# Loading x turned by DMA instead of turning it on TensorE, in an attention and mixture-of-experts kernel

## The reference, cut to what matters

```
x = x + xattn(layernorm(x), k, bias, ctx, ctx, 8)
xt = layernorm(x).reshape(2048, 256)
scores = softmax(xt @ Wg.T)                    # 16 experts in 4 groups
topi = the 4 best experts within the 2 best groups
h = silu(xt @ W1[e].T) * (xt @ W3[e].T)        # 176 wide, for each chosen expert e
y = sum over the 4 of scores[e] * (h @ W2[e].T)
z = the same with shared weights, 352 wide, for every token
x = x + y + z
```

## Time and profile before

| what | us |
|---|---|
| median of 3 runs | 399.13 |
| lowest, highest | 397.67, 399.59 |
| the profiled execution's span | 395.4 |
| TensorE busy | 384.7 |
| VectorE busy | 244.1 |
| GpSimd busy | 180.3 |
| ScalarE busy | 162.9 |

### The profile page before, as it was taken

The page is one execution under the profiler, slowest core; times in us unless marked ns, Lnnn a source line. Parts: engine busy times, 40 slices in busy tenths (PEclk is TensorE's granted clock), DMA queues, the critical chain, the costliest instruction groups (busy, mean ns, idle before and its releaser), DMA issues.

```text
span 395.4 us, 9070 instructions
## 1 busy us (share of the span) xinstructions
PE 384.7 (97%) x2146; PEld 279.3 (71%) x2147; DVE 244.1 (62%) x676; ACT 162.9 (41%) x494; POOL 180.3 (46%) x225
## 2 busy tenths in 40 slices
PE   6999999999999999999999999999999999999996
PEld 6788888888888546555667675446767777777765
DVE  3577577987988465788735344443445464646466
ACT  5347656564564362101124333333333333334431
POOL 3254323337888573565553333333333333334333
PEclk9999999999999999999999999999999999999999
DMA  7974474368879996256376873334474737362737
GB/s 248 363 254 139 163 277 144 133 206 278 309 250 335 414 419 258 96 207 223 104 215 219 321 239 107 87 95 134 127 246 136 242 115 242 115 232 103 264 97 251
DMA packets 37812, 83.09 MB, mean 210 GB/s; under 512 B 5930, under 2 KB 25870, under 8 KB 35728
## 3 DMA queue, kind: packets, MB, share of 16 engines
q1 hardware_dynamic: 31248, 64.83, 49.1%
q0 software_dynamic: 6528, 17.84, 11.6%
HBM read 60.21 MB, written 23.48 MB: 212 GB/s over the span
## 4 chain that ended last, share of the span: by engine, by line
PE 79%; DVE 10%; DMA 4%; issue 2%; ACT 2%; SPq 1%; DVEq 1%; POOL 0%; POOLq 0%
PE heads L1382 18%; PE bank L1456 13%; PE heads L1271 11%; PE heads L1424 7%; PE heads L1273 5%; PE bank L1437 5%; PE heads L1392 4%; PE bank L1403 4%; PE bank L1285 3%; DVE kv L734 3%; PE heads L1374 3%; DMA toep<-toep_in 2%; PE bank L1448 2%; DVE prod L763 2%; DMA y_scratch<-toep,dest_i 2%
## 5 line engine op out<-in xcount | busy, mean ns | idle before, releaser
L716 POOL DMA_INDIRECT y_scratch<-toep,dest_i x72 | 71.8, 997 | 112.0 <-DVE dest_i L1131 96.0
L1382 PE MATMUL heads<-experts,toep 128*128 x256 | 86.6, 461 | 0.6 <-DVE toep L1089 0.5
L1271 PE MATMUL heads<-toep,kv 128*128 128x256 f32 x256 | 77.9, 386 | 1.9 <-DVE kv L734 0.8
L661 POOL DMA_INDIRECT rows_scratch<-rows,slot_i x64 | 63.3, 989 | 35.4 <-issue 19.5
L1456 PE MATMUL bank<-experts,toep 88*128 x256 | 66.2, 381 | 1.6 <-DVE toep L1096 1.6
L553 ACT ACTIVATE toep<-heads 128x176 f32<-128x176 f32 x72 | 22.8, 317 | 78.1 <-PE heads L1382 67.2
L1382 PEld LDWEIGHTS heads<-experts,toep 128*128 128x128 f32 x256 | 43.7, 190 | 14.8 <-issue 1.1
L1273 PEld LDWEIGHTS heads<-toep,kv 128*128 128x128 f32 x256 | 48.7, 190 | 6.5
L763 DVE TENSOR_TENSOR prod<-heads,ctx_rep 128x1024 f32<-128x1024 f32 x32 | 39.1, 1221 | 22.3 <-PE bank L1285 19.9
L1096 DVE COPY toep<-heads 88x256 f32<-88x256 f32 x72 | 30.2, 419 | 31.1 <-PE heads L1392 31.1
L1273 PE MATMUL heads<-toep,kv 128*128 128x128 f32 x256 | 49.2, 274 | 0.0
(11 more groups left out here) (240 smaller groups left out, 513.4 us busy)
## 6 DMA issues: line engine op xcount, KB each, us to landing
ctx_rep<-ctxr_in SPq DMA_DIRECT2D x16, 1024.0 KB, 5.0
experts<-experts_in SPq DMA_DIRECT2D x16, 608.0 KB
toep<-rows_scratch SPq DMA_DIRECT2D x56, 144.0 KB
prod<-y_scratch SPq DMA_DIRECT2D x5, 1024.0 KB, 5.5
rows_scratch<-pad_row SPq DMA_DIRECT2D x17, 144.0 KB, 1.8
ctx_tr<-ctxt_in SPq DMA_DIRECT2D x16, 128.0 KB
toep<-toep_in SPq DMA_DIRECT2D x4, 512.0 KB, 7.0
ctx_n<-ctx_in SPq DMA_DIRECT2D x16, 128.0 KB, 2.1
```

Source lines behind the costliest of these rows:

```text
L661: pool.indirect_dma_start(rows_d, bass.IndirectOffsetOnAxis(ap=slot_i[:, u, k:k + 1].bitcast(U32), axis=0), rows[:, u, :], None).then_inc( ...
L716: pool.indirect_dma_start(y_d, bass.IndirectOffsetOnAxis(ap=dest_i[b][:, 0:1].bitcast(U32), axis=0), y_sb[b], None, bounds_check=TOPK * TO ...
L1271: nc.tensor.matmul(y_ps[par][:, i, :], kv[:, q, 0, h * P:(h + 1) * P], toep[:, q * HH + h, :], start=True, stop=False)
L1382: last = nc.tensor.matmul(up_ps[p], x_tr[p][:, blk, :], up_w(e, blk), start=blk == 0, stop=blk == LB - 1)
```

## The change

The rows are scattered in another layout, and loaded turned.

- After `norm2`, which now writes into `xn`, ScalarE runs one more instruction for each unit (`split_row`): it splits the 256 float32 numbers of a row into 256 lower and 256 upper halves of 16 bits, side by side in `rows`. The scatter moves the same 1152 bytes per row.
- `gather` issues a DMA transpose of the 128 rows x 512 halves, which lands as 4 blocks of 128 x 128 halves, and a second, plain DMA of the 32 gates per row, with a semaphore of its own. A mixed tile takes two of each, a late tile one of each.
- `turn_x` on TensorE is gone, and its PSUM banks. `src_tr` on ScalarE no longer copies from PSUM but weaves the lower and upper halves in SBUF into float32, 512 halves per partition, and waits for the DMA instead of for TensorE.

```
+            def turned(mem, at, lo, count):
+                return sp.dma_start_transpose(in_halves(mem).rearrange("p (r n) -> p r n", n=P)[:, :, lo:lo + count],
+                                              halves_d[bass.ds(at, count), 0:2 * L])
             def gather(t, b, before):
                 if not (isinstance(t, int) and t < DEPTH):
-                    sp.wait_ge(xtr_ps, t - (DEPTH - 1))
+                    sp.wait_ge(xtr_ready, t - (DEPTH - 1))
                     sp.wait_ge(taken, t - (DEPTH - 1))
...
                 if is_mixed(t):
-                    sp.dma_start(xg[b][0:HALF], rows_d[bass.ds(at, HALF)]).then_inc(rows_in[b], 16)
+                    turned(xg[b], at, 0, HALF).then_inc(rows_in[b], 16)
+                    sp.dma_start(xg[b][0:HALF, L:], rows_d[bass.ds(at, HALF), L:]).then_inc(gates_in[b], 16)
...
                 else:
-                    sp.dma_start(xg[b], rows_d[bass.ds(at, P)]).then_inc(rows_in[b], 16)
+                    turned(xg[b], at, 0, P).then_inc(rows_in[b], 16)
+                    sp.dma_start(xg[b][:, L:], rows_d[bass.ds(at, P), L:]).then_inc(gates_in[b], 16)
...
+            def split_row(u):
+                act.wait_ge(xn_ready, u + 1)
+                nc.scalar.activation(in_halves(rows[:, u, :]).rearrange("p (s l) -> p s l", s=2),
+                                     xn_of(u).bitcast(U16).rearrange("p (l s) -> p s l", s=2), ACT.Copy
+                                     ).then_inc(row_ready, 1)
...
-            def src_tr(w, p):
+            def src_tr(w, p, b, before):
                 if not (isinstance(w, int) and w < 2):
                     act.wait_ge(up_done, w - 1)
-                act.wait_ge(xtr_ps, w + 1)
-                nc.scalar.activation(x_tr[p], xt_ps[p], ACT.Copy).then_inc(xtr_ready, 1)
+                rows_landed(act, w, b, before)
+                nc.scalar.activation(x_tr[p].rearrange("p b n -> p (b n)").bitcast(U16).rearrange("p (n s) -> p n s", s=2),
+                                     in_halves(rows_of(w, b)).rearrange("p (s n) -> p n s", s=2), ACT.Copy
+                                     ).then_inc(xtr_ready, 1)
...
             def routed_step(t, b, before):
                 up(t, p, b)
-                if not (isinstance(t, int) and t == LIVE - 1):
-                    turn_x(t + 1, 1 - p, (b + 1) % DEPTH, before + 1 if b == DEPTH - 1 else before)
```

More of the change, by code:

```diff
@@ L27 @@
 I32 = mybir.dt.int32
+U16 = mybir.dt.uint16
 U32 = mybir.dt.uint32
@@ L102, in build @@
         resid = sb("resid", [P, UNITS, L])
+        xn = sb("xn", [P, L])
         rows = sb("rows", [P, UNITS, ROW])
@@ L110, in build @@
         ident = sb("ident", [P, P])
+        blocks = xn[:, 0:P]
         sum_i = sb("sum_i", [P, 2, 32])
-        blocks = sb("blocks", [P, P])
         skip_w = sb("skip_w", [P, 2, P])
@@ L221, in build @@
         s_up, s_silu, s_hid, s_down = sem("shared_up"), sem("shared_silu"), sem("shared_hid"), sem("shared_down")
-        rows_in = [sem(f"rows_in{b}") for b in range(DEPTH)]
-        xtr_ps, xtr_ready, up_done, silu_done, hid_ready, ht_done, htr_ready, dn_done = (
-            sem("xtr_ps"), sem("xtr_ready"), sem("up_done"), sem("silu_done"), sem("hid_ready"), sem("ht_done"),
+        rows_in, gates_in = ([sem(f"{n}_in{b}") for b in range(DEPTH)] for n in ("rows", "gates"))
+        xtr_ready, up_done, silu_done, hid_ready, ht_done, htr_ready, dn_done = (
+            sem("xtr_ready"), sem("up_done"), sem("silu_done"), sem("hid_ready"), sem("ht_done"),
             sem("htr_ready"), sem("dn_done"))
@@ L227, in build @@
         y_sent = [sem(f"y_sent{b}") for b in range(DEPTH)]
-        late_in = [sem(f"late_in{j}") for j in range(LATE)]
+        late_in, late_gates = ([sem(f"{n}{j}") for j in range(LATE)] for n in ("late_in", "late_gates"))
         sends_ready, unit_ps, unit_ready = sem("sends_ready"), sem("unit_ps"), sem("unit_ready")
@@ L232, in build @@
         other_in = [sem(f"other_in{g}") for g in range(MIXED)]
-        others_in = [sem(f"others_in{b}") for b in range(DEPTH)]
+        others_in, other_gates = ([sem(f"{n}{b}") for b in range(DEPTH)] for n in ("others_in", "other_gates"))
         added, finished = sem("added"), sem("finished")
@@ L237, in build, with xn_of @@
         block = ctx.enter_context(nc.Block())
+        def xn_of(u):
+            return spread[:] if u == UNITS - 1 else xn[:]
         def v_forward(q):
@@ L274, in rows_of, with in_halves @@
             return rows[:, UNITS - LIVE + t, :] if is_late(t) else xg[b]
+        def in_halves(mem):
+            return mem[:, 0:L].bitcast(U16)
         def rows_landed(eng, t, b, before):
@@ L281, in rows_landed, with gates_landed @@
                 eng.wait_ge(rows_in[b], before * 16 + 16)
+            if is_mixed(t):
+                eng.wait_ge(others_in[b], (t - MIXED0) // DEPTH * 16 + 16)
+        def gates_landed(eng, t, b, before):
+            if is_late(t):
+                eng.wait_ge(late_gates[t - LIVE + LATE], 16)
+            else:
+                eng.wait_ge(gates_in[b], before * 16 + 16)
+            if is_mixed(t):
+                eng.wait_ge(other_gates[b], (t - MIXED0) // DEPTH * 16 + 16)
         def is_mixed(t):
@@ L363, in gather @@
                 if is_mixed(t):
-                    sp.dma_start(xg[b][0:HALF], rows_d[bass.ds(at, HALF)]).then_inc(rows_in[b], 16)
+                    turned(xg[b], at, 0, HALF).then_inc(rows_in[b], 16)
+                    sp.dma_start(xg[b][0:HALF, L:], rows_d[bass.ds(at, HALF), L:]).then_inc(gates_in[b], 16)
                     also = sp.value_load(other_row[0:1, t - MIXED0:t - MIXED0 + 1], min_val=0, max_val=E * REGION + HALF)
-                    sp.dma_start(xg[b][HALF:P], rows_d[bass.ds(also, HALF)]).then_inc(others_in[b], 16)
-                else:
-                    sp.dma_start(xg[b], rows_d[bass.ds(at, P)]).then_inc(rows_in[b], 16)
+                    turned(xg[b], also, HALF, HALF).then_inc(others_in[b], 16)
+                    sp.dma_start(xg[b][HALF:P, L:], rows_d[bass.ds(also, HALF), L:]).then_inc(other_gates[b], 16)
+                else:
+                    turned(xg[b], at, 0, P).then_inc(rows_in[b], 16)
+                    sp.dma_start(xg[b][:, L:], rows_d[bass.ds(at, P), L:]).then_inc(gates_in[b], 16)
             def load_other(g):
@@ L409, in late_gather @@
                 at = sp.value_load(tile_row[0:1, t:t + 1], min_val=0, max_val=E * REGION)
-                sp.dma_start(rows[:, UNITS - LATE + j, :], rows_d[bass.ds(at, P)]).then_inc(late_in[j], 16)
+                mem = rows[:, UNITS - LATE + j, :]
+                turned(mem, at, 0, P).then_inc(late_in[j], 16)
+                sp.dma_start(mem[:, L:], rows_d[bass.ds(at, P), L:]).then_inc(late_gates[j], 16)
             others_at = {5: (0,), 7: (1,), 8: (2,), 9: (3,), 10: (4,), 11: (5,), 13: (6,), 14: (7,)}
@@ L501, in norm2 @@
                 act.wait_ge(b2, u + 1)
-                nc.scalar.activation(rows[:, u, 0:L], resid[:, u, :], ACT.Identity,
-                                     bias=ln2[:, u, 4:5], scale=ln2[:, u, 3:4]).then_inc(row_ready, 1)
+                if 1 <= u < UNITS - 1:
+                    act.wait_ge(xt_done, u)
+                nc.scalar.activation(xn_of(u), resid[:, u, :], ACT.Identity,
+                                     bias=ln2[:, u, 4:5], scale=ln2[:, u, 3:4]).then_inc(xn_ready, 1)
+            def split_row(u):
[3 more added lines that the diff above has]
+                                     ).then_inc(row_ready, 1)
             def copy_xn(u):
@@ L538, in _ @@
                     norm1(u + 2)
+                if u >= 2:
+                    split_row(u - 2)
                 if u >= ROUTE0 and (u - ROUTE0) % TB == 0:
                     exponentials((u - ROUTE0) // TB)
-            def src_tr(w, p):
+            def src_tr(w, p, b, before):
                 if not (isinstance(w, int) and w < 2):
                     act.wait_ge(up_done, w - 1)
-                act.wait_ge(xtr_ps, w + 1)
-                nc.scalar.activation(x_tr[p], xt_ps[p], ACT.Copy).then_inc(xtr_ready, 1)
+                rows_landed(act, w, b, before)
+                nc.scalar.activation(x_tr[p].rearrange("p b n -> p (b n)").bitcast(U16).rearrange("p (n s) -> p n s", s=2),
+                                     in_halves(rows_of(w, b)).rearrange("p (s n) -> p n s", s=2), ACT.Copy
+                                     ).then_inc(xtr_ready, 1)
             def silu(w, p):
@@ L581, in _ @@
             copy_xn(UNITS - 1)
+            split_row(UNITS - 2)
             silu_shared(2)
+            split_row(UNITS - 1)
             copy_logits(UNITS - 1)
@@ L587, in _ @@
                 silu_shared(s)
-            src_tr(0, 0)
+            src_tr(0, 0, 0, 0)
             def routed_step(t, b, before):
@@ L593, in routed_step @@
                 if not (isinstance(t, int) and t == LIVE - 1):
-                    src_tr(t + 1, 1 - p)
+                    src_tr(t + 1, 1 - p, (b + 1) % DEPTH, before + 1 if b == DEPTH - 1 else before)
```

(11 more changed lines are left out.)

8 lines of the change are left out of this document (3 added, 5 removed).

## The result

The changed kernel took 479.35 us in the median of 4 runs (477.5 to 481.78), against 399.06 for the kernel before: a ratio of 1.204, with an interval of 1.201 to 1.208. I had forecast 417 with a range to 468: right in the direction and the mechanism, wrong in the size.

A forecast was written before the change was run, and what follows sets the result against it. TensorE bounded the kernel before; SP would bound the changed one. SP's added 44.5 + 16.0 us, less 36.6 of waits, put tile 63's up product 19.7 later: span 395.4 + 19.7 - 1.8 = 413.3, plus 3.7 outside, 417 us; range 401 to 468.

The forecast's parts named there:

- SP as the second bound: Routed tiles, kernel before: SP works some 125 of 163 us, 23% below TensorE, the first bound.
- the gates alone using up its free time: SP's separate gate loads add 44.5 us, more than the 37.6 us in which SP waited.
- x, SP's price for issuing a transpose: SP's issue cost of a transpose beyond a plain load: 0.2 us, 80 times, 16.0 us; bounds 0 and 1.0.
- 481 for x = 1.0: Rival of dear transposes: SP held 1.0 us longer per transpose gives 481 us; chance 0.17, clock rival included.
- The gate load: SP's second DMA per tile: 0.53 us for ordinary and late loads, 0.665 for each half of a mixed tile.
- ScalarE "fits, within 0.05": Routed tiles: woven x ready 0.85 us after the up product, in time for TensorE's next weight load, at no cost.
- The bound of 0.77: Upper bound on ScalarE's weaving time; it would cost 0.15 us a tile with TensorE as the bound, nothing with SP.
- rival 2: Routed tiles: TensorE stays the bound, so the kernel gets faster, 383.3 us at best, 391 with half; chance 0.07.
- The end.: After SP's last load, done at 379.7: tile 63's up product starts at 382.4, 19.7 us later than before.
- Landing and DMA engines: Late loads' transposes land in 3.0 us; transposes cost the 16 DMA engines nothing more than plain loads.
- the bound of 1.2: Upper bound on a transpose's extra DMA engine time: all 16 are full at 1.2 us above the load it replaces.
- The clock: Rival: TensorE's clock falls to 0.92 in the routed stage, tiles take 2.48 us, SP's pace covers it; within a 0.17 chance.

The follow-up runs named there:

- The split load: The kernel before, with each tile's row load split into one DMA for the 256 numbers and one for the 32 gates, TensorE still turning x: 414.03 us.
- the two kernels with plain loads: The changed kernel with plain DMAs in place of its transposes, 416.75 us; the kernel before with its load split into numbers and gates, 414.03 us.
- the unturned load: The changed kernel with one plain DMA per tile of the whole rows, gates included, and no turning of x anywhere: 396.40 us, ratio 0.9965.

## Why the prediction was wrong in size

**SP as the second bound, and the gates alone using up its free time: right.** The split load shows it without any transpose, at 414 us.

**x, SP's price for issuing a transpose: mis-sized, and the step that failed.** I took 0.2 us, from the extra 0.056 and 0.079 of patterns with one more loop, three times. It measured 1.209 - 0.333 = 0.876 on the 64 ordinary and late loads. On the 16 halves of the mixed tiles it is less, since a plain load of 64 rows costs 0.47 to issue and the transpose 1.18: 0.71. Together 64 x 0.676 + 16 x 0.51 = 51.4 us of the 62 that were missing. The upper bound, 1.0 from the longest single issue, did hold it. I put the high end of the range between the bounds, at 468, on the ground that only one issue of sixteen was that long, which says nothing about a transpose. The method failed too: from 1 to 4 blocks the issue goes from 1.123 to 1.208 us, so the price is not made of pieces, and rows of plain DMAs, with however many loops, could not have shown it. With the measured x the prediction's sum gives 417 + 51.4 = 468.4. That its 481 for x = 1.0 lies so near the measured 479 is luck: the terms below make up the rest.

**The gate load: 0.53 a tile, measured 0.64** (330.86 to 331.50). Behind a transpose its issue takes 0.422, behind a plain DMA 0.333 as in the two kernels with plain loads. 64 x 0.11 = 7.0 us; in the mixed tiles it is 0.70 for 0.665, 0.6 us more.

**ScalarE "fits, within 0.05": wrong.** I had weaving ready 0.85 us after the up product and wanted by 0.89. Weaving took 0.685, not 0.6, and I left out the 0.14 from its end to the weight load, and that this load would no longer lie beside the matmuls. The bound of 0.77 with "0.15 a tile" was nearer. In the changed kernel it shows above all behind SP's last load: up of tile 63 starts at 443.32, of tile 71 at 464.28, 20.96 us where I had 8 x 2.28 = 18.2. It would have cost nearly the whole gain had SP not been the bound, so rival 2, TensorE as the bound at 383, was not to be had in this order even with free issues: the unturned load gives 396.

**The end.** From SP's last instruction to the up product of tile 63 I had 2.7 us, and it was 443.32 - 438.1 = 5.2. The rows were not late: the transpose of tile 63 went out at 436.28, and the weaving of its rows, from 442.37, did not wait for a DMA. TensorE was late. At 426.67 SP had issued a read-back of 1 MB; the transpose behind it, issued at 428.18, landed only 4.3 us later, and TensorE stood still for 4.10 us. Then its granted clock was 0.50, from 432 to 438 us. The timeline of ScalarE and TensorE there, and windows with the granted clock and the DMA share as their last but two and last but one numbers (the share adds up packet times and can pass 1):

```profile
432.52 0.69 ACT L588 ACTIVATE toep<-toep 128x512 uint16<-128x512 uint16 x1 [3.90 <-DMA toep<-rows_scratch]
433.45 2.71 PE L1426 MATMUL heads<-experts,toep 128*128 x4 [4.10 <-ACT toep L588]
430.00:432.00 2.00, 0.00 (x0) 0.00 (x0) 0.09 (x1) 0.00 (x0) 0.18 (x1) 0.84 1.14 364
434.00:436.00 2.00, 2.00 (x5) 1.05 (x4) 0.17 (x1) 0.00 (x0) 0.98 (x1) 0.50 0.35 80
438.00:440.00 2.00, 2.00 (x10) 1.49 (x9) 1.28 (x5) 0.76 (x3) 0.81 (x1) 0.95 0.23 48
```

Tile 60, from its up product at 433.45 to the next at 438.30, took 4.85 us at a clock of 0.50, where a tile at 1.00 takes 2.63. These 2.2 us are most of the 2.5. The first load went out at 195.5, 1.1 us later than before. I took this for the cost of the first part, but no run shows it: with the same first part and the two instructions on ScalarE exchanged, the first load went out at 194.55. Together 51.4 + 7.6 + 2.8 + 2.5 + 1.1 = 65.4, less 0.7 because SP's waits fell to 0.3 and not to 1: 64.7, against 476.9 - 413.3 = 63.6 in the profiled spans. The 3.7 us that I added for what lies outside of the span was 2 too many: every run lies 1.7 to 1.8 above its own span (478.67 against 476.9), and the profiled execution before was quicker than the median.

**Landing and DMA engines: right that they do not set the pace, wrong that a transpose costs them nothing more.** The transposes landed in 2.6 us, and the same loads as plain DMAs in 2.1. The queue that carries them keeps the engines busy for 45.9% of 476.9 us, against 47.5% of 415.0 us with plain loads of the same bytes: 218.9 against 197.1 us, so a transpose costs 0.27 us more, between my nothing and the bound of 1.2. All queues together fill the engines to 45% from 300 to 440 us. No row or run had shown a transpose when I took nothing; it was an assumption, at the lower bound. What counted was the issue, 1.209 us for 0.333.

**The clock: right that it does not set SP's pace, wrong that it costs nothing.** Its mean fell to 0.85 from 300 to 440 us, further than the 0.92 that I had taken, and SP's waits were 0.3 us from 193 to 440 us. At the end, at 0.50, it cost the 2.2 us above.

## What to carry to other kernels

An engine that only issues DMAs has no busy time on the page; before giving it one more instruction a tile, add up its instructions with their gaps and compare with its waits. Where a change moves work from the bounding engine to another, follow the ring through the other engine's order, with every hand-over and with the weight load that is hidden now, and ask what stands ahead of the moved work in that order. An operation that the trace does not show should keep both of its bounds in the range, above all where its price counts 80 times.

## What the runs showed of the hardware

- A DMA transpose holds SP for 1.12 us (16 rows x 128 16-bit numbers) to 1.21 us (128 rows x 512), and for between 1.16 and 1.21 in the six sizes between, against 0.33 for a plain DMA of 128 rows. It landed in 2.6 us in the median of 16, where the same loads as plain DMAs took 2.1.
- A plain DMA of 128 rows that follows a transpose was issued in 0.42 us instead of 0.33; one of 64 rows in 0.49 instead of 0.47.
- A transposed load took 0.27 us more of the 16 DMA engines' time than a plain one of the same bytes.
- ScalarE takes 0.685 us to copy 512 16-bit numbers per partition from SBUF to SBUF, where a silu of 512 float32 from PSUM took 0.597.
- A stationary operand that comes late costs TensorE about 0.24 us that an early one does not. The profile shows it as a longer matmul group (1.43 for 1.19), and as idle time of the weight load put down to "issue", not as a wait for ScalarE.
- TensorE stood still for 4.10 us, up to 433.45. Its granted clock was 1.00 from 420 to 430 us, 0.50 from 432 to 438, and 0.95 from 438 to 440, after it had been busy without a gap from 434 on. A tile took 4.85 us at 0.50 and 2.63 at 1.00.
